# All four partition quarters of the adjacency loads issued from SyncE's queue

## The reference

```python
h  = item_feat @ W_item.T + b_item                     # 10000 x 128
x1 = layernorm(x + relu(adj @ h + x @ W_user.T + b_user))
Wh = x1 @ W                                            # 128 x 128 W
e  = leaky_relu((Wh @ a[:128]) + (Wh @ a[128:]).T, 0.2)
at = softmax(where(adj > 0, e, -9e15), axis=1)
out = layernorm(x1 + elu(at @ Wh))
```

## Time and profile before

| | |
|---|---|
| profiled execution, its own time | 2799.53 us |
| its span, first to last instruction | 2797.5 us |
| median of the runs | 2799.47 us |
| TensorE busy | 2746.7 us (98%) |
| VectorE busy | 2439.3 us (87%) |
| ScalarE busy | 889.2 us (32%) |
| queue q1 (SP) | 239.32 MB |
| queue q10 (ScalarE) | 228.15 MB |
| mean granted TensorE clock | 0.994 |

### The profile page before, as it was taken

One profiled execution on the slowest core, in us unless ns is written; L12 is line 12 of the kernel. 1 busy time (PEld: TensorE's weight loads), 2 busy tenths in 40 slices (PEclk: granted clock), 3 DMA queues, 4 the chain that ended last, 5 costly groups with the idle time before them and its releaser, 6 DMA issues.

```text
span 2797.5 us, 22810 instructions
## 1 busy us (share of the span) xinstructions
PE 2746.7 (98%) x6955; PEld 1280.3 (46%) x6955; DVE 2439.3 (87%) x2654; ACT 889.2 (32%) x710; POOL 3.5 (0%) x33
## 2 busy tenths in 40 slices
PE   7999999999999999999989999999999999999997
PEld 5444444444444444444544444444444444444454
DVE  3888888888888888888889898989898989898987
ACT  2555555555555555555550010101010101010111
POOL 0000000000000000000000000000000000000000
PEclk9999999999999999999999999999999999999999
DMA  9999999999999999999880000000000101010000
GB/s 237 323 312 326 306 313 315 315 315 313 315 314 318 312 317 311 316 312 324 257 227 0 19 16 19 15 19 15 19 25 9 34 0 34 0 34 0 15 8 13
DMA packets 340292, 468.18 MB, mean 167 GB/s; under 512 B 57880, under 2 KB 174856, under 8 KB 340104
## 3 DMA queue, kind: packets, MB, share of 16 engines
q1 hardware_dynamic: 202008, 239.32, 29.7%
q10 hardware_dynamic: 138224, 228.15, 26.9%
HBM read 443.85 MB, written 23.55 MB: 167 GB/s over the span
## 4 chain that ended last, share of the span: by engine, by line
PE 96%; DMA 2%; DVE 1%; ACTq 0%; issue 0%; ACT 0%; SPq 0%; DVEq 0%
PE bank L512 46%; PE bank L552 24%; PE bank L553 23%; DMA area_r<-in_adj_dram 1%; PE bank L510 1%; PE bank L490 1%; PE bank L540 1%; DMA area_p<-in_L_gnn_item_feat_dram 1%; DVE adj_t L596 0%; ACTq L291 0%; PE bank L466 0%; DMA area_r<-s_scratch 0%; PE bank L458 0%; DMA b_user_col<-in_L_gnn_b_user_dram 0%; DMA s_scratch<-ts_row 0%
## 5 line engine op out<-in xcount | busy, mean ns | idle before, releaser
L512 PE MATMUL bank<-adj_t,area_h 128*128 128x512 f32 (+1 forms) x3160 | 1335.4, 583 | 3.5 <-DVE adj_t L596 3.5
L596 DVE STREAM_TRANSPOSE adj_t<-area_r 128x2048 f32<-128x2048 f32 (+3 forms) x400 | 892.5, 2231 | 177.4 <-PE bank L512 89.9
L848 DVE SCALAR_TENSOR_TENSOR adj_t<-area_r,c_col,area_h 128x1024 f32<-128x1024 uint8 (+2 forms) x790 | 954.1, 1256 | 104.5 <-PE bank L553 103.5
L512 PEld LDWEIGHTS bank<-adj_t,area_h 128*128 128x128 f32 x3160 | 597.8, 190 | 718.3 <-issue 707.3
L950 ACT ACTIVATE mask_out<-adj_t 128x4096 uint8<-128x4096 f32 (+1 forms) x200 | 699.9, 3501 | 648.8 <-DVE packing L670 371.5
L552 PE MATMUL bank<-adj_t,area_r 128*128 128x512 f32 x1580 | 807.8, 593 | 9.2 <-DVE adj_t L848 9.2
L553 PE MATMUL bank<-adj_t,area_r 128*128 128x512 f32 (+1 forms) x1580 | 775.9, 573 | 0.0
L553 PEld LDWEIGHTS bank<-adj_t,area_r 128*128 128x128 f32 x1580 | 300.5, 190 | 378.4 <-issue 378.4
L552 PEld LDWEIGHTS bank<-adj_t,area_r 128*128 128x128 f32 x1580 | 299.6, 190 | 351.3 <-issue 333.5
L781 DVE TENSOR_TENSOR area_h<-area_p,bit_of 128x2048 uint32<-128x2048 uint32 (+1 forms) x100 | 220.9, 2209 | 0.0
L1072 ACT COPY area_h<-bank 128x512 f32<-128x512 f32 x10 | 5.9, 586 | 469.1 <-PE bank L553 469.1
(11 more groups left out here) (121 smaller groups left out, 465.0 us busy)
## 6 DMA issues: line engine op xcount, KB each, us to landing
area_r<-in_adj_dram SPq DMA_DIRECT2D x312, 512.0 KB, 10.0
area_r<-in_adj_dram ACTq DMA_DIRECT2D x312, 512.0 KB, 10.6
area_r<-in_adj_dram SPq DMA_DIRECT2D x78, 480.0 KB, 8.8
area_r<-in_adj_dram ACTq DMA_DIRECT2D x78, 480.0 KB, 8.6
mask_scratch<-packed ACTq DMA_DIRECT2D x40, 320.0 KB, 9.4
area_p<-mask_scratch SPq DMA_DIRECT2D x20, 640.0 KB, 6.1
x_scratch<-area_s ACTq DMA_DIRECT2D x20, 256.0 KB, 8.6
area_h<-x_scratch SPq DMA_DIRECT2D x10, 512.0 KB, 4.0
```

What stands on the lines that cost most here:

```text
L512: mm = nc.tensor.matmul(acc1[par][:, 0:live], h[:, c * SPC + s, :], adj_t[:, c % 2, s * width:s * width + live], start=(c == 0 and s == 0) ...
L596: nc.vector.transpose(dst, src).then_inc(half_turned, 1)
L848: nc.vector.scalar_tensor_tensor(out=prob[:, n, 0:width], in0=lhs, scalar=c_col[:, b:b + 1], in1=unpacked[:, c % 2, n, 0:width // 4].bitca ...
```

## The change

The four quarters of every adjacency unit are issued by SyncE, one after the other, on q1. ScalarE issues none; its function `loads_ahead` and the parameter that it needed go, and with them the special last blocks of its loop. `load_adjacency` itself, the slots, the semaphores and their counts are as they were. The stores, and ScalarE's half of the `item_feat` loads, stay on q10.

```diff
             for c in range(1, NC):
                 load_item(sp, c, (0, 1))
                 if c == 4:
-                    load_adjacency(sp, 0, 0, IB, (0, 1))
+                    load_adjacency(sp, 0, 0, IB, range(A))
                 if c == 6:
-                    load_adjacency(sp, 0, 1, IB, (0, 1))
+                    load_adjacency(sp, 0, 1, IB, range(A))
             load_x(0, IB)
             for u in range(2, RAW):
-                load_adjacency(sp, 0, u, IB, (0, 1))
+                load_adjacency(sp, 0, u, IB, range(A))
...
-                    load_adjacency(sp, k, u, width, (0, 1))
+                    load_adjacency(sp, k, u, width, range(A))
...
-                if c == 2:
-                    load_adjacency(act, 0, 0, IB, (2, 3))
-                if c == 4:
-                    load_adjacency(act, 0, 1, IB, (2, 3))
...
-            for u in range(2, RAW):
-                load_adjacency(act, 0, u, IB, (2, 3))
...
-            def loads_ahead(k, c, nxt):
-                for u in (c + RAW - 1, c + RAW):
-                    if u < UPB:
-                        load_adjacency(act, k, u, IB if nxt else TW, (2, 3))
-                    elif nxt:
-                        load_adjacency(act, k + 1, u - UPB, nxt, (2, 3))
...
-            def layer1(k, par, width, first, nxt=IB):
+            def layer1(k, par, width, first):
                 for c in range(NC):
-                    if c % 2 == 1:
-                        loads_ahead(k, c, nxt)
                     mask_chunk(k, c, width)
...
-            with act.Fori(3, NB - 3, 2) as k:
+            with act.Fori(3, NB - 1, 2) as k:
                 layer1(k, 1, IB, False)
                 layer1(k + 1, 0, IB, False)
-            layer1(NB - 2, 1, IB, False)
-            layer1(NB - 1, 0, IB, False, TW)
-            layer1(NB, 1, TW, False, 0)
+            layer1(NB, 1, TW, False)
```

## The result

The changed kernel takes 3328.32 us (median of four runs, 3325.68 to 3331.51), the kernel before 2799.69: a ratio of 1.1887, interval 1.1873 to 1.1901. It is 529 us slower. The forecast was 3286, 42 us too low. The profiled execution took 3328.9 us, its span is 3327.0.

What follows compares the result with a forecast made beforehand. TensorE was taken to bound the kernel, SP's queue layer 1 after the change: start 15.5, adjacency 1839, x 30, item loads 6, stores 3, passage 30, layer 2 and end 1362.4, together 3286 us; range 2975 to 3430.

Steps and rivals of the forecast that it cites:

- The bound changes hands: Layer 1: pace passes from TensorE to SP's queue, about 96 us a block instead of 69.67.
- ScalarE's issues are worth nothing: Taking 400 adjacency issues, some 150 us, off ScalarE's instruction queue gains 0, as ScalarE isn't on the chain.
- SP's issuing costs nothing: SP issuing 800 instead of 400 adjacency loads, 13 to 15 us of a block's 69.67, costs 0.
- The mechanism, halves and not queues: Adjacency loads: writing only partitions 0 to 63, or only 64 to 127, at once limits the rate to about 220 GB/s.
- One ground: Early adjacency stretch of the earlier trace: SP's queue alone gave 225 GB/s over 8 us, ScalarE having nothing queued.
- the second half: Later part of load_right's 11 us in the earlier trace, quarters written in turn from SP's queue: about 200 to 225 GB/s.
- The sum: Whole kernel: start, adjacency, x, item loads, stores, passage and layer 2 added to 3286 us, 17% slower.
- the passage: From layer 1 to layer 2's first matmul: 30 us, between 26 and 35, against 34.8 before.
- a gain of 0.4 us a unit where the halves turn: Adjacency on SP's queue: both halves written briefly at each turn, making a unit 9.5 us, 220 GB/s.
- A: Rival for layer 1's adjacency: engines drift apart and write both halves, 2850 to 3110 us; chance 0.16.
- B: Rival for layer 1: one queue gives 301 GB/s or more, TensorE sets the pace, 2799.5 us; chance 0.06.
- C's clock: Layer 1: TensorE's clock may halve after gaps, costing nothing unless half throughout, over 4000 us; C's chance 0.06.

Runs made afterwards that it cites:

- e5: Changed kernel, but each full adjacency DMA spreads its rows over all 128 partitions instead of one quarter: 2796.79 us, ratio 0.9982 to the kernel before.
- e6: Changed kernel, but each adjacency DMA spreads its rows over 64 partitions of one half: 3326.37 us, ratio 1.1875 to the kernel before.
- e7: Changed kernel, but per unit quarter 0 alone, two DMAs across partitions 32 to 95, then quarter 3 alone: 3056.41 us, ratio 1.0920 to the kernel before.
- e3: Changed kernel with SP issuing the quarters in the order 0, 2, 1, 3: 3266.70 us, ratio 1.1658 to the kernel before.
- e4: Changed kernel with quarter order 0, 2, 1, 3 twice a unit, each DMA cut in two: 3175.30 us, ratio 1.1340 to the kernel before.
- e1: Kernel before, but SP issues quarters 0 and 2, ScalarE 1 and 3, both starting in the same half: 3105.54 us, ratio 1.1087.
- e2: Kernel before, but SP issues quarters 0 and 2, ScalarE 3 then 1, starting in opposite halves: 3082.69 us, ratio 1.1007.
- e10: Kernel before, but SP issues quarters 0, 2 and ScalarE 3, 1, each waiting until the unit two before has landed: 2976.37 us, ratio 1.0615.
- e11: Kernel before, but SP issues quarters 0, 2 and ScalarE 1, 3, each waiting until the unit two before has landed: 3222.00 us, ratio 1.1515.

## Why the prediction was right

**The bound changes hands.** Right. 301 GB/s were wanted, one queue gave 215, and layer 1 went with the bytes: 97.6 us a block (forecast 96).

**ScalarE's issues are worth nothing, and SP's issuing costs nothing.** Right. VectorE and ScalarE do the same work in the same busy time (2439 and 889 us, before and after); e5 has the same 800 issues on SP and is not slower than before.

**The mechanism, halves and not queues.** Right, and shown by e5 (one queue, all partitions: the loss is gone), e6 (wider in one half: all of it there) and e7 (half of the DMAs across the middle: half of it there).

The Trainium skill's SBUF — State Buffer, section Door 1: The DMA port swizzle, gives this order (0 to 63 hardly better than 0 to 31, both with an asymptote of about 218 GB/s), and e6 and the changed kernel agree, with 214.9 GB/s on q1 in each. The same page of the Trainium skill, section "Can I just issue two DMAs to hit both halves?", says that they serialize, with 6% gained; here two queues in two halves made 350 GB/s against 212 to 217 of one alone, and the measurement decides.

**One ground was stated wrongly.** I wrote of the earlier trace rows that ScalarE had nothing queued. It had: six adjacency DMAs were issued from 49.94 us on, and no packet of theirs ran before about 56 us. The queues of the kernel before, from 49.5 to 55.5 us, show the issues, with 16.8 us to landing, and q1's packets alone:

```profile
DMA packets 652, 1.28 MB, mean 213 GB/s; under 512 B 36, under 2 KB 36, under 8 KB 651
...
q1 hardware_dynamic: 651, 1.26, 106.2%
...
area_r<-in_adj_dram ACTq DMA_DIRECT2D x6, 512.0 KB, 16.8
```

The reading of the rate stands (only q1's packets moved), but the stretch is not one of an idle second queue. And of the earlier trace rows I wrote that the second half runs at about 200 to 225 GB/s; its last four slices, where the loads run out, fall from 186 to 108. Nothing rested on these four.

**The sizes.** The sum was 43 us short of the profiled execution. Adjacency, x, the item loads on q1 and the stores were put at 1839 + 30 + 6 + 3 = 1878 us, so the last adjacency load should have landed at 1893.5 us. The last one was issued at 1925.3 and landed 12.6 us later:

```profile
L291 SPq DMA_DIRECT2D area_r<-in_adj_dram x1: 449/449/449, 1925.3 to 1925.3; - x1
...
DMA to landing us min/median/max: 12.6/12.6/12.6
```

That is 1937.9 us, 44 us late. From there to the first matmul of layer 2 it is 28.8 us, and the passage was put at 30; layer 2 was as before. (Counted from the first mask load, as the rows do, the passage took 40.9 us: its first mask loads are issued with the last adjacency units still in the queue, and from 1925 to 1935 us they show 15.2 us to landing, where the page's median for them is 6.3. I had left this overlap out of the sum.)

```profile
area_p<-mask_scratch SPq DMA_DIRECT2D x3, 640.0 KB, 15.2
```

The term that was mis-sized is the adjacency: I took 220 GB/s, by a gain of 0.4 us a unit where the halves turn. From 1335.8 to 1386.6 us, with adjacency alone on the queues, q1 moved 216 GB/s:

```profile
DMA packets 5772, 10.98 MB, mean 216 GB/s; under 512 B 342, under 2 KB 1442, under 8 KB 5772
...
q1 hardware_dynamic: 5772, 10.98, 107.1%
```

At that rate 404.5 MB take 1873 us, 34 more than the 1839 of the sum: the changed kernel stays at the rows' 212 to 217 GB/s, and most of the gain for its two turns a unit isn't there, though e3 and e4 show that more turns are worth something. The other 10 us lie in x, the item loads and the stores; no run parts them.

**The rivals.** A (drift of the engines over both halves) would have needed over 240 GB/s; it stayed at 225 with stores. B fell with the same number, though e5 reached it by another way. C's clock: 0.90 of full on the average, L512's matmuls 628 ns instead of 583, and TensorE busy 80% instead of the 73% I gave. It hid in the gaps, as forecast: TensorE still waited 304.4 us for VectorE's L596, and the time is the one that the bytes give.

## What to carry to other kernels

Where loads are split into DMAs that each write a part of the partitions, look at which halves are written at the same time, before counting queues: a fixed assignment of one half to each queue kept TensorE fed (314 GB/s in the kernel before), and one queue whose DMAs span all 128 partitions did as well (315 GB/s in e5). A busy share of the DMA engines near 1 doesn't say that they move what they can; put GB/s beside it, and look for stretches in which one queue runs alone, since they tell what it can do. If a single queue must do it, alternate the halves from DMA to DMA and keep the DMAs small; both together brought back 29% of the loss here, the order alone 12%.

## What the runs showed of the hardware that I had not expected

A queue with issued DMAs got no packet through for 6 us while the other had a backlog (the rows above of 49.5 to 55.5 us). Why wasn't tried.

Two queues that change halves didn't stay in step by themselves: e1 and e2, opposite by design, took the same time within their spread, and it took a wait for landed units to part the two orders by 246 us (e10, e11).

The same 2 KB pieces at 314 and 315 GB/s took a DMA share of 1.05 from two queues with a half each (the kernel before, 300 to 1300 us), and of 0.90 from one queue over all partitions (e5). I can't say from these runs whether the queue or the spread does it.
